# Cross-attention over projected tokens: the score matmuls in halves of 64 rows, with the other engines' order around them

## What is computed

```python
q = _split_heads(hidden_states @ w_q, HEADS)
k = _split_heads(text @ w_k, HEADS)
v = _split_heads(text @ w_v, HEADS)
out_text = _merge_heads(_sdpa(q, k, v))
k_ip = _split_heads(ip_h @ w_k_ip, HEADS)
v_ip = _split_heads(ip_h @ w_v_ip, HEADS)
out_ip = _merge_heads(_sdpa(q, k_ip, v_ip, mask=mask_ip))
out = out_text + IP_SCALE * out_ip
out = out @ w_out + b_out
out = out + residual
```

## Time and profile before

| | us |
|---|---|
| median of three runs | 881.52 |
| the profiled execution | 881.16 |
| its span, first to last instruction | 879.4 |
| TensorE busy (weight loads apart) | 874.3 |
| weight loads | 752.0 |
| VectorE busy | 723.2 |
| ScalarE busy | 591.2 |
| GpSimd busy | 524.3 |

### The profile page before, as it was taken

One profiled execution on the slowest core, in us unless ns is written; L12 is line 12 of the kernel. 1 busy time (PEld: TensorE's weight loads), 2 busy tenths in 40 slices (PEclk: granted clock), 3 DMA queues, 4 the chain that ended last, 5 costly groups with the idle time before them and its releaser, 6 DMA issues.

```text
span 879.4 us, 13951 instructions
## 1 busy us (share of the span) xinstructions
PE 874.3 (99%) x4716; PEld 752.0 (86%) x4716; DVE 723.2 (82%) x1017; ACT 591.2 (67%) x986; POOL 524.3 (60%) x421
## 2 busy tenths in 40 slices
PE   9999999999999999999999999999999999999998
PEld 8899888888888888888888888888888888888877
DVE  6779889797888879797887879787897978888785
ACT  7766685857767585765768486675858577574773
POOL 1059677392846649293755739375664929466581
PEclk9999999999999999999999999999999999999999
DMA  9924223011030403003030301204030210301011
GB/s 315 358 100 135 83 76 127 1 68 68 1 127 1 134 0 106 21 2 132 0 127 0 134 0 37 90 0 134 0 127 0 76 58 0 119 23 39 1 48 72
DMA packets 34203, 64.63 MB, mean 73 GB/s; under 512 B 4480, under 2 KB 6784, under 8 KB 34048
## 3 DMA queue, kind: packets, MB, share of 16 engines
q1 hardware_dynamic: 33888, 62.84, 21.1%
q10 hardware_dynamic: 288, 1.44, 0.4%
HBM read 40.34 MB, written 23.59 MB: 73 GB/s over the span
## 4 chain that ended last, share of the span: by engine, by line
PE 97%; DVE 2%; POOL 1%; ACT 1%; issue 0%; POOLq 0%
PE bank L95 25%; PE bank L97 25%; PE bank L96 25%; PE bank L1131 8%; PE bank L1151 4%; PE bank L1152 4%; PE bank L1040 1%; PE bank L1046 1%; PE bank L1043 1%; DVE total L225 1%; PE bank L1061 1%; PE bank L1058 1%; PE bank L1093 0%; DVE top L219 0%; PE bank L1083 0%; POOL prob L178 0%
## 5 line engine op out<-in xcount | busy, mean ns | idle before, releaser
L512 POOL TENSOR_TENSOR oT_lo<-o_raw,oT_hi 128x512 fp32r<-128x512 f32 x78 | 101.1, 1296 | 226.0 <-ACT oT_hi L681 225.9
L178 POOL TENSOR_TENSOR prob<-prob,top 128x1120 f32<-128x1120 f32 x126 | 177.7, 1440 | 0.0
L184 POOL TENSOR_TENSOR prob<-prob,inv 128x1120 f32<-128x1120 f32 x126 | 177.2, 1441 | 0.0
L95 PE MATMUL bank<-xT_hi,wq_hi 128*128 128x512 f32 x400 | 162.9, 407 | 0.0
L919 DVE TENSOR_TENSOR o_raw<-bank,pv_part 64x512 f32<-64x512 f32 x160 | 110.2, 689 | 62.6 <-ACT pv_part L677 60.1
L95 PE MATMUL bank<-oT_hi,wo_hi 128*128 128x512 f32 (+1 forms) x405 | 157.4, 389 | 0.0
L96 PE MATMUL bank<-oT_lo,wo_hi 128*128 128x512 f32 (+1 forms) x405 | 156.7, 387 | 0.0
L97 PE MATMUL bank<-oT_hi,wo_lo 128*128 128x512 f32 (+1 forms) x405 | 156.6, 387 | 0.0
L97 PE MATMUL bank<-xT_hi,wq_lo 128*128 128x512 f32 x400 | 156.5, 391 | 0.0
L96 PE MATMUL bank<-xT_lo,wq_hi 128*128 128x512 f32 x400 | 155.9, 390 | 0.0
L677 ACT ACTIVATE pv_part<-bank 64x512 f32<-64x512 f32 x160 | 94.9, 593 | 62.7 <-PE bank L1152 60.1
(11 more groups left out here) (121 smaller groups left out, 1695.2 us busy)
## 6 DMA issues: line engine op xcount, KB each, us to landing
xin<-in_xT SPq DMA_DIRECT2D x16, 1280.0 KB, 6.8
outT<-res SPq DMA_DIRECT2D x79, 256.0 KB, 6.8
w_raw<-in_L_xattn_w_k SPq DMA_DIRECT2D x8, 320.0 KB, 5.4
w_raw<-in_L_xattn_w_k_ip SPq DMA_DIRECT2D x8, 320.0 KB, 5.8
w_raw<-in_L_xattn_w_v_ip SPq DMA_DIRECT2D x8, 320.0 KB, 3.6
w_raw<-in_L_xattn_w_v SPq DMA_DIRECT2D x8, 320.0 KB, 3.5
v_raw<-v_scratch SPq DMA_DIRECT2D x14, 140.0 KB
prob<-in_textT SPq DMA_DIRECT2D x8, 224.0 KB, 5.0
```

Source lines behind the costliest of these rows:

```text
L95: nc.tensor.matmul(dst, a_hi, b_hi, start=first, stop=False)
L178: ins = eng.tensor_tensor(s, s, top[:, t, n, :].unsqueeze(2).broadcast_to([P, HEADS, k1 - k0]), ALU.subtract)
L184: ins = eng.tensor_tensor(s, s, inv[:, t, n, :].unsqueeze(2).broadcast_to([P, HEADS, k1 - k0]), ALU.mult)
L512: nc.gpsimd.tensor_tensor(oT_lo[:, m, :], o_raw[:, m % 2, :], oT_hi[:, m, :].bitcast(F32), ALU.subtract).then_inc(oT_lo_done, 1)
```

## The change

The score matmuls are cut in two by rows. `k_parts` holds the keys in blocks of two heads: 64 rows, 128 columns. A step of 128 features is now three pairs of matmuls, one on rows 0 to 63 and one on rows 64 to 127, each of 128 moving columns, into two banks. Four steps (`RUN`) fill the two banks of one `score_units`, so five such runs make the ten units; six banks, 0 to 5, take them in turn, and run 2 waits for the value product's last addition (`pv_added`). ScalarE's copy writes 128-column pieces at the places where they belong. A tile of 128 queries now needs 4, 6, 8 and 10 copied units.

GpSimd no longer makes the last output remainder (VectorE does, at the head of its `softmax`), and its third mask moves behind the first subtraction. VectorE's output additions and x remainders are put in another order. The transposes of the first two head pairs are issued query tile by query tile. In group 0 the text values wait for all copied scores. The setup zeroes one key buffer of the same size in place of two.

```diff
-        k_hi, k_lo = sb("k_hi", [P, KD, HPT, KEYS], F32R), sb("k_lo", [P, KD, HPT, KEYS], F32R)
+        k_parts = sb("k_parts", [P, KD, 2, PW], F32R)
...
-        s_bank, t_bank, v_bank = bank[0:4], bank[2:4], bank[4:6]
+        s_bank, t_bank, v_bank = bank[0:6], bank[2:4], bank[4:6]
...
         def units_for_tile(t):
-            return -(-(t + 1) * SW // 512)
+            return 2 * -(-(t + 1) * KD // RUN)
...
-        def score_unit(pe, g, n, b, new_batch):
-            if n < 2:
+        def score_dst(n):
+            steps = prob[:, n // 2 * RUN * CW:(n // 2 + 1) * RUN * CW].rearrange("p (i r c) -> p r i c", r=2, c=PW)
+            return steps[:, n % 2, :, :]
+
+        def score_units(pe, g, u, b, new_batch):
+            if u == 0:
                 wait(pe, score_copied, UNITS * g)
-            elif n < 4:
+            elif u == 1:
                 wait(pe, pT_lo_done, PAIRS * g)
+            elif u == 2:
+                wait(pe, pv_added, PAIRS * g)
             else:
-                pe.wait_ge(score_copied, UNITS * g + n - 3)
-            if n == 0 and new_batch:
+                pe.wait_ge(score_copied, UNITS * g + 2 * u - 4)
+            if u == 0 and new_batch:
                 pe.wait_ge(k_built, HPT * (b + 1))
-            for half in range(2):
-                t, m = divmod(2 * n + half, KD)
+            for i in range(RUN):
+                t, m = divmod(RUN * u + i, KD)
                 if t == 0:
                     pe.wait_ge(q_lo_done, KD * g + m + 1)
                 q_cols = slice(t * P, (t + 1) * P)
-                keys = [k[:, m, :, :].rearrange("p j k -> p (j k)") for k in (k_hi, k_lo)]
-                ins = three(s_bank[n % 4][:, half * CW:(half + 1) * CW], qT_hi[:, m, q_cols], qT_lo[:, m, q_cols], *keys, True, True)
-            ins.then_inc(score_ready, 1)
+                for n, (q, part) in enumerate(((qT_hi, 0), (qT_hi, 1), (qT_lo, 0))):
+                    for r in range(2):
+                        rows = slice(r * HP, (r + 1) * HP)
+                        ins = nc.tensor.matmul(s_bank[(2 * u + r) % 6][:, i * PW:(i + 1) * PW], q[rows, m, q_cols], k_parts[rows, m, part, :], start=n == 0, stop=n == 2)
+                        if i == RUN - 1 and n == 2:
+                            ins.then_inc(score_ready, 1)
...
                 def softmax(g):
                     add_mask(pool, g, 0)
-                    oT_part(g - 1, KD - 1)
                     add_mask(pool, g, 1)
-                    add_mask(pool, g, 2)
                     for t in range(GT):
                         sub_max(pool, g, t, 1)
-                        if t == 0:
-                            add_mask(pool, g, 3)
+                        if t < 2:
+                            add_mask(pool, g, t + 2)
...
+                def last_oT_part(g):
+                    dve.wait_ge(oT_lo_done, KD * g + KD - 1)
+                    dve.wait_ge(oT_hi_done, KD * (g + 1))
+                    nc.vector.tensor_tensor(oT_lo[:, KD - 1, :], o_raw[:, (KD - 1) % 2, :], oT_hi[:, KD - 1, :].bitcast(F32), ALU.subtract).then_inc(oT_lo_done, 1)
...
-                    for t in range(GT):
+                    last_oT_part(g - 1)
+                    maxima(dve, g, 0)
+                    maxima(dve, g, 1)
+                    split_x(0, 2)
+                    for t in (2, 3):
                         maxima(dve, g, t)
-                        if t == 2:
-                            split_x(0, 2)
-                    output(g - 1, 1 - u, 0)
-                    for t in range(GT):
-                        split_x(t + 2, min(t + 3, KD))
-                        if t in (1, 2):
+                        output(g - 1, 1 - u, t - 2)
+                    for t in range(GT - 1):
+                        if t > 0:
                             output(g - 1, 1 - u, t + 1)
+                        split_x(t + 2, t + 3)
                         sums(dve, g, t)
-                        if t not in (1, 2):
-                            output(g - 1, 1 - u, t + 1)
+                    output(g - 1, 1 - u, KD - 1)
+                    sums(dve, g, GT - 1)
...
                         if k == 0 and n % 2 == 0:
-                            pe.wait_ge(score_copied, UNITS if n == 0 else UNITS - 2)
+                            pe.wait_ge(score_copied, UNITS)
...
                 def values(g, b, new_batch):
-                    p_transpose(g, 0)
-                    p_transpose(g, 1)
+                    pe.wait_ge(score_copied, UNITS * (g + 1))
+                    for t in range(GT):
+                        pe.wait_ge(prob_done, GT * g + t + 1)
+                        for p in range(2):
+                            ins = transpose_tile(g, p, t)
+                            if t == GT - 1:
+                                ins.then_inc(pT_ready, 1)
```

More of the change, by code:

```diff
@@ L40, in attention_kernel @@
     CW = HPT * KEYS
+    PW = 2 * KEYS
+    RUN = 512 // PW
     SW = HEADS * KEYS
@@ L127, in q_lo_part, with k_head @@
             nc.vector.tensor_tensor(qT_lo[:, m, :], l_bank[(m + 1) % 2][:], qT_hi[:, m, :].bitcast(F32), ALU.subtract).then_inc(q_lo_done, 1)
-        def k_head(t, j):
-            return t[j * DH:(j + 1) * DH, :, j, :]
+        def k_head(part, j):
+            return k_parts[j * DH:(j + 1) * DH, :, part, j % 2 * KEYS:(j % 2 + 1) * KEYS]
         def k_hi_part(act, b, raw=None):
@@ L136, in k_hi_part @@
             for j in range(HPT):
-                nc.scalar.activation(k_head(k_hi, j), raw[j * DH:(j + 1) * DH], ACT.Copy).then_inc(k_hi_built, 1)
+                nc.scalar.activation(k_head(0, j), raw[j * DH:(j + 1) * DH], ACT.Copy).then_inc(k_hi_built, 1)
         def k_lo_part(dve, b, raw=None):
@@ L200, in score_unit, with copy_scores @@
                 q_cols = slice(t * P, (t + 1) * P)
-                keys = [k[:, m, :, :].rearrange("p j k -> p (j k)") for k in (k_hi, k_lo)]
-                ins = three(s_bank[n % 4][:, half * CW:(half + 1) * CW], qT_hi[:, m, q_cols], qT_lo[:, m, q_cols], *keys, True, True)
-            ins.then_inc(score_ready, 1)
-        def copy_scores(act, g, u):
-            act.wait_ge(score_ready, UNITS * g + u + 1)
-            nc.scalar.activation(prob[:, u * 512:(u + 1) * 512], s_bank[u % 4][:], ACT.Copy).then_inc(score_copied, 1)
+                for n, (q, part) in enumerate(((qT_hi, 0), (qT_hi, 1), (qT_lo, 0))):
[4 more added lines that the diff above has]
+                            ins.then_inc(score_ready, 1)
+        def copy_scores(act, g, n):
+            act.wait_ge(score_ready, UNITS * g + n + 1)
+            nc.scalar.activation(score_dst(n), s_bank[n % 6][:].rearrange("p (i c) -> p i c", c=PW), ACT.Copy).then_inc(score_copied, 1)
         def exponentials(act, g, t, shared):
@@ L481, in _ @@
                                         pattern=[[-1, P]], channel_multiplier=1).then_inc(ident_made, 1)
-                for buf in (k_hi, k_lo):
-                    nc.gpsimd.memset(buf[:].rearrange("p m j k -> p (m j k)").bitcast(F32), 0.0).then_inc(k_zeroed, 1)
+                nc.gpsimd.memset(k_parts[:].rearrange("p m s c -> p (m s c)").bitcast(F32), 0.0).then_inc(k_zeroed, 1)
                 mine = pool_chunks
@@ L625, in _ @@
                 act.dma_start(k_scratch.rearrange("p b n -> p (b n)"), k_all.rearrange("p b m k -> p (b m k)")).then_inc(k_stored, 16)
-                act.wait_ge(k_zeroed, 2)
+                act.wait_ge(k_zeroed, 1)
                 k_hi_part(act, 0, k_all[:, 0, :, :])
@@ L989, in last_values @@
                             pT_part(g, n)
-                    dve.wait_ge(oT_lo_done, KD * NG - 1)
-                    dve.wait_ge(oT_hi_done, KD * NG)
-                    nc.vector.tensor_tensor(oT_lo[:, KD - 1, :], o_raw[:, (KD - 1) % 2, :], oT_hi[:, KD - 1, :].bitcast(F32), ALU.subtract).then_inc(oT_lo_done, 1)
+                    last_oT_part(g)
                 def values(g, build=False):
@@ L1113, in _ @@
                         ins.then_inc(k_ipT_ready, 1)
-                for n in range(UNITS):
-                    score_unit(pe, 0, n, 0, True)
+                for u in range(UNITS // 2):
+                    score_units(pe, 0, u, 0, True)
                 for k in range(KC):
@@ L1133, in p_transpose @@
                 def p_transpose(g, p):
[L1134 to L1137, removed]
+                    pe.wait_ge(pT_lo_done, PAIRS * g + p - 1)
                     for t in range(GT):
-                        if p == 0:
-                            pe.wait_ge(prob_done, GT * g + t + 1)
                         ins = transpose_tile(g, p, t)
@@ L1192, in scores @@
                 def scores(g, b, new_batch):
-                    for n in range(UNITS):
-                        score_unit(pe, g, n, b, new_batch)
+                    for u in range(UNITS // 2):
+                        score_units(pe, g, u, b, new_batch)
                     for m in range(KD):
@@ L1215, in last_group @@
                 def last_group(g, b):
-                    for n in range(UNITS):
```

(3 more changed lines are left out.)

2 lines of the change are left out of this document (1 added, 1 removed).

## The result

The changed kernel takes 919.49 us (four runs, 918.43 to 920.4), against 881.59 us before: 1.043 times as long, 95% interval 1.042 to 1.044. The forecast was 877.1 us, in a range from 857 to 898. So it missed by 42 us, and on the wrong side.

A forecast was written before the change was run, and what follows sets the result against it. The prediction took TensorE's back-to-back matmuls to bound the kernel. Scores over 14 middle groups (-4.9 us), group 0 (+0.45) and the last group (0) made -4.45 us: 877.1 us from a median of 881.52, range 857 to 898.

The forecast's parts named there:

- The part that seemed least certain: TensorE's scores: the two half loads run side by side, 110 ns a pair, stage 6.83 us, 0.35 us less.
- rival D: TensorE's score pairs: two loads queue on one weight path, 110 + 110 ns; +100 us, 981 us; chance 0.17.
- the switch: TensorE changing between whole array and row halves around the scores: 0.23 us a group, bounds 0 and 0.39 us.
- Group 0: First text values wait for all ten score copies: +0.8 us, against -0.35 of the stage, +0.45 us.
- the last group: TensorE waits 0.63 us for VectorE's normalisation there, so a shorter score stage gives nothing: 0.
- VectorE's new order: Reordered output additions and x remainders: could move VectorE about 2 us either way, up to 1.5 us for TensorE; taken as 0.
- the step on GpSimd: GpSimd's softmax: no gap after the first subtraction, ending 30.2 us into the group, 0.45 us to spare, no cost.
- Rival E: Scores as forecast, but VectorE late in seven key-building groups: 7 x 1 us lost, 884 us; chance 0.13.
- rival C: TensorE's score pairs: loads side by side, streams one after the other, 132 ns; +15 us, 896 us; chance 0.10.
- rival B: TensorE's score pairs limited by streaming, 66 ns, with the softmax unable to follow: 22 us gained, 859 us; chance 0.17.

The follow-up runs named there:

- e3_swap: The changed kernel with the x remainder ahead of the output addition in the loop over the sums; 879.69 us, 0.9968 of the kernel before.
- e1_order_only: The kernel before with only VectorE's new order of output additions, x remainders and maxima; 896.3 us, 1.015 times the kernel before.
- e7_swap_first: The changed kernel with the x remainder ahead of the output addition at the second query tile's sums only; 895.38 us.
- e4_halves_only: The kernel before with score halves and six banks alone, all orders old, oT_lo on GpSimd; 883.11 us, 1.0011 of the kernel before.
- e9_old_masks: e2_old_order with GpSimd's third mask ahead of the first subtraction again; 883.0 us, 1.0011 of the kernel before.
- e6_half_by_half: e3_swap with twelve matmuls on one row half, then twelve on the other; 1036.12 us in a single run.
- e10_short_moving: e3_swap with 64 instead of 128 moving columns in two of the three matmuls of each product; 941.14 us in a single run.
- e2_old_order: The changed kernel with VectorE's old order, oT_lo staying at its head with VectorE; 919.38 us.

## Why the prediction was wrong

**What held.** The part that seemed least certain came out close: 112 ns a pair (110), a stage of 6.84 us (6.83), rival D out of the question. That the stage agrees to the hundredth is luck: the 6.83 held the switch on the way in, which the 6.84 does not; with it the stage is 6.93 us. The two loads of a pair begin together: the changed kernel's weight loads in order of time have two (x2) in the 0.19 us of one.

```profile
438.59 0.19 PEld L214 LDWEIGHTS bank<-k_parts,qT_lo 64*128 64x128 f32 x2
```

The switch costs 0.09 us going in (438.38, where 438.06 + 0.227 was due). A group of e3_swap is 50.44 - 50.19 = 0.25 us shorter than before and not 0.35, since I had counted that gap as part of the stage. The first mask starts 442.74 - 438.38 = 4.36 us into the stage (4.5), the first subtraction 6.54 us (6.6). Group 0 lost 66.05 - 65.38 = 0.67 us (0.45). With both collisions gone, e3_swap stands at 879.7 us, 2.6 us above the forecast: 1.4 us for the gap, 0.2 for group 0, 0.4 us for the last group, whose transposes begin 21.27 us after its scores instead of 20.82, where I had written 0; of the remaining 0.6 us, 0.4 is the level of that set of runs, in which the kernel before took 881.9 us and not 881.5, and 0.2 is not accounted for.

**What failed** is one term, VectorE's new order: "So the order can move VectorE by about 2 us either way ... I take 0". It was 1.65 us twice in each of the 14 groups; the bound beside the 0 was 1.5 us in the seven key-building groups only. With it failed the step on GpSimd, "From there GpSimd runs on without a gap ... Still 0.45 us to spare": GpSimd had two gaps of 1.65 us, and ended at 466.24 + 5.43 = 471.67, 33.3 us into the group instead of 30.2. I had the row that shows it, the 2.58 us of one remainder in the earlier trace rows, and left it as noise "beside GpSimd's work". Laid against GpSimd's rows it would have shown its partner: in the kernel before, the only slow remainder of that group, at 436.81, starts just behind GpSimd's text subtraction of 436.76, and the quick one, at 441.79, stands right behind the reciprocal and meets only GpSimd's short instruction (GpSimd and VectorE of the kernel before, in order of time).

```profile
436.76 2.07 POOL L178 TENSOR_TENSOR prob<-prob,top 128x1120 f32<-128x1120 f32 x1
441.79 0.63 DVE L109 TENSOR_TENSOR xT_lo<-xin,xT_hi 128x512 fp32r<-128x512 f32 x1
```

That collision was with a subtraction and cost TensorE nothing. In the new order both later remainders come among the normalisations, each behind an output addition of 0.6 us. For the second remainder that addition is new, and it stands between the reciprocal, which releases GpSimd after the first collision, and the remainder: GpSimd begins at 461.65, the remainder 0.38 us later. The first collision is not tied in this way: GpSimd comes to 457.06 from its subtractions without a wait, and the remainder is 0.04 us behind it. In e1_order_only it was 0.38 us ahead, and was over in 0.97 us. Nor does the second need the release: e7_swap_first has it without the first, at 551.36.

**Rival E** named the right engine and the wrong cause. It let VectorE be late by its later start, priced that at 7 x 1 us, and gave it 0.13. Its mechanism is real, and about half the size, in the two runs with VectorE's old order: in e4_halves_only and e9_old_masks the key-building groups wait for the remainder of q and take 50.7 us against 50.2. In e3_swap, which starts as late, TensorE waits for nobody in the middle groups. What it missed is that both engines lose: GpSimd's wait lengthens the softmax, TensorE's slack of 0.76 us is used up, and all groups pay, 2.9 us in the mean (53.10 against 50.19): 2.2 us where no keys are built, 3.4 us where they are.

**The range** took in a loss of 16 us at most, from rival C. The bound that the row gave for this term, two slow remainders of 2 us in 14 groups, was 56 us; it was not carried into the range. Two sums beside this are off, without weight for the result: rival B takes a wait of 1.4 us where its own 29.8 less 28.0 give 1.8, so it would come to about 865 us and not 859; and with the 0.23 us of the switch the change breaks even at 116 ns a pair, not at rival D's 120.

## What to carry to other kernels

When an order of VectorE's instructions changes, find for each one with two SBUF inputs which GpSimd instruction it will meet, and in particular whether the instruction before it releases GpSimd: put such an operation ahead of the release or directly behind it, and an operation that reads PSUM, or a reduction, into the time that follows. One slow instance among equal instructions in a trace may be a collision with a partner; look for the partner before taking it for noise. And a reordering can be worth ten times the arithmetic it was made for: here 0.25 us a group gained on TensorE, 2.9 us lost beside it, and one exchanged pair of lines gave all of it back.

## What the runs showed of the hardware

Two row halves load and multiply at once: 112 ns for a pair of 64-row matmuls, against 112 ns for each where they follow on one half (e6_half_by_half).

The granted clock can fall while TensorE never waits. In the changed kernel it stays at 1.0 through the stage. In the group of e10_short_moving shown above it is at 1.0 (2.4 GHz) until about 341.5 and then at 0.50 (1.2 GHz), with TensorE issuing pairs without a gap all the time; the place differs from group to group (in the group from 718.43 it falls near 723.9). In e6_half_by_half, where for most of the stage only one half works at a time, it falls at about 315.8 in the group shown. Before it fell, the array had been given fewer columns (64 in two of three pairs) or half the rows at a time. The output projection that follows pays too: from 347.90 to 351.50 it still runs at 0.50, and only in the next window is it back.

```profile
347.90:351.50 3.60, 3.60 (x11) 2.83 (x10) 1.87 (x3) 3.51 (x6) 3.08 (x3) 0.50 0.00 0
351.50:360.00 8.50, 8.50 (x39) 7.06 (x38) 6.80 (x11) 5.10 (x7) 5.43 (x4) 0.98 0.00 0
```

Which of the two made it fall, the columns or the rows in use, was not separated. It falls after waits as well: in e2_old_order behind a wait of 1.8 us in seven of 14 groups, where it adds 1.6 us to the group. A wait of TensorE can cost more than its own length.
